# Transposed scores in two column halves, in a two-layer gated attention and feed-forward kernel

## The reference

```python
# _L0_xattn_ref, bs = 16, sq = sk = 64
q = (query @ wq).reshape(bs, sq, 32, 128).transpose((0, 2, 1, 3))
k = (key @ wk)  # 8 heads, each repeated for 4 query heads
v = (value @ wv)
q = _apply_rope(q, 0)
k = _apply_rope(k, 0)
raw = jnp.einsum('bhqd,bhkd->bhqk', q, k) / scale
masked = raw + mask[:bs, None, 0:sq, :sk]
attn = jax.nn.softmax(masked, axis=-1)
out = jnp.einsum('bhqk,bhkd->bhqd', attn, v)
...
return out @ wo
# caller
x = x + jnp.tanh(g_xattn[0]) * _L0_xattn_ref(_layernorm(x), ctx, ctx, mask, ...)
x = x + jnp.tanh(g_ffn[0]) * _L0_ffn_ref(_layernorm(x), ...)    # 4-bit weights, 8-bit activations
x = x + jnp.tanh(g_xattn[1]) * _L1_xattn_ref(_layernorm(x), ctx, ...)
x = x + jnp.tanh(g_ffn[1]) * _L1_ffn_ref(_layernorm(x), ...)    # experts picked by index `active`
```

## Time and profile before

| what | us |
|---|---|
| median of 3 runs (lowest, highest) | 801.29 (799.98, 801.77) |
| the profiled execution, whole | 801.0 |
| its span in the trace | 799.0 |
| PE busy | 788.0 |
| DVE busy | 586.8 |
| ACT busy | 446.9 |
| POOL busy | 503.3 |
| PE busy in the span from 300 to 560 us | 259.39 of 260.00 |

### The profile page before, as it was taken

How to read it: one execution, slowest core, us unless ns; L and a number is a source line. 1 busy time by engine, 2 the same in 40 slices (tenths; PEclk the granted TensorE clock), 3 DMA queues, 4 the chain that set the end, 5 groups by cost and what they waited for, 6 DMA issues and landing times.

```text
span 799.0 us, 13826 instructions
## 1 busy us (share of the span) xinstructions
PE 788.0 (99%) x5060; PEld 645.4 (81%) x5060; DVE 586.8 (73%) x1097; ACT 446.9 (56%) x844; POOL 503.3 (63%) x429
## 2 busy tenths in 40 slices
PE   8999999999999999999999999999999999999997
PEld 7888888888888888888888888888765777777776
DVE  5867988668888654686666565565899988998873
ACT  4754555444445434444445443333579898888773
POOL 1697577745766764566666456645457885887762
PEclk9999999999999999999999999999999999999999
DMA  9411331432333231733212110166273413213101
GB/s 304 134 67 47 98 94 41 126 77 57 93 90 91 63 102 31 52 90 93 87 40 68 49 45 27 33 75 251 90 190 100 107 48 86 67 48 80 48 15 40
DMA packets 72258, 66.76 MB, mean 84 GB/s; under 512 B 35920, under 2 KB 51504, under 8 KB 71808
## 3 DMA queue, kind: packets, MB, share of 16 engines
q1 hardware_dynamic: 71520, 65.56, 31.8%
q10 hardware_dynamic: 672, 0.33, 0.1%
HBM read 49.04 MB, written 6.34 MB: 69 GB/s over the span
## 4 chain that ended last, share of the span: by engine, by line
PE 93%; DVE 4%; ACT 1%; POOL 1%; DMA 1%; issue 1%; SPq 0%; DVEq 0%
PE bank L87 12%; PE bank L88 11%; PE bank L89 11%; PE bank L532 7%; PE bank L527 7%; PE bank L528 7%; PE bank L509 7%; PE bank L653 4%; PE bank L1660 4%; PE bank L1646 3%; PE bank L1612 2%; PE bank L1583 2%; PE bank L1591 2%; PE bank L640 2%; PE bank L1636 2%; PE bank L1637 2%
## 5 line engine op out<-in xcount | busy, mean ns | idle before, releaser
L963 DVE SCALAR_TENSOR_TENSOR x_res<-bank,gate,x_res 128x512 f32<-128x512 f32 x128 | 94.1, 744 | 67.6 <-PE bank L532 67.3
L1249 POOL TENSOR_TENSOR prob<-prob,row_inv 128x512 f32<-128x512 f32 x32 | 33.5, 1048 | 162.4 <-DVE row_inv L959 162.4
L1235 POOL TENSOR_TENSOR rope_swap<-rope_swap,trig 128x512 f32<-128x512 f32 x80 | 105.9, 1323 | 35.0 <-ACT rope_swap L722 34.7
L721 ACT COPY rope_swap<-bank 64x512 f32<-64x512 f32 x80 | 46.8, 585 | 106.8 <-DVE rope_cos L934 106.7
L87 PE MATMUL bank<-xnT_hi,wq_hi 128*128 128x512 f32 x256 | 103.0, 402 | 0.0
L527 PE MATMUL bank<-wo_hi,oT_hi 128*128 128x512 f32 x256 | 101.7, 397 | 1.2 <-DVE x_res L963 0.6
L88 PE MATMUL bank<-xnT_lo,wq_hi 128*128 128x512 f32 x256 | 101.4, 396 | 0.0
L89 PE MATMUL bank<-xnT_hi,wq_lo 128*128 128x512 f32 x256 | 101.2, 395 | 0.0
L528 PE MATMUL bank<-wo_lo,oT_hi 128*128 128x512 f32 x256 | 100.8, 394 | 0.0
L934 DVE TENSOR_TENSOR rope_cos<-bank,trig 128x512 f32<-128x512 f32 x80 | 54.6, 682 | 61.2 <-PE bank L89 61.1
L1241 POOL TENSOR_TENSOR q_rope<-rope_cos,rope_swap 128x512 f32<-128x512 f32 x64 | 84.4, 1319 | 5.0
(11 more groups left out here) (259 smaller groups left out, 2017.8 us busy)
## 6 DMA issues: line engine op xcount, KB each, us to landing
wq_raw<-in_L_xattn_wq SPq DMA_DIRECT2D x16, 512.0 KB, 4.2
wo_raw<-in_L_xattn_wo SPq DMA_DIRECT2D x16, 512.0 KB, 3.9
xn<-in_L_ffn_Wd SPq DMA_DIRECT2D x16, 256.0 KB, 3.2
b_ctx<-in_ctx SPq DMA_DIRECT2D x32, 128.0 KB, 2.6
b_k_twice<-b_qk_hi SPq DMA_DIRECT2D x32, 128.0 KB, 2.4
w_T_dram<-w_out SPq DMA_DIRECT2D x28, 128.0 KB, 2.7
w_T<-w_T_dram SPq DMA_DIRECT2D x2, 1376.0 KB, 17.9
xn<-in_L_ffn_Wg SPq DMA_DIRECT2D x10, 256.0 KB, 3.8
```

What stands on the lines that cost most here:

```text
L963: dve.scalar_tensor_tensor(out=K.x[:, t, :], in0=wo_ps[t % 2][:, :], scalar=K.gate[:, 0:1], in1=K.x[:, t, :], op0=ALU.mult, op1=ALU.add).t ...
L1235: pool.tensor_tensor(out=sw, in0=sw, in1=sin_b, op=ALU.mult).then_inc(s_rope, 1)
```

## The change

It has four parts.

- Scores of units 1 to 31 (`scoreT_unit`) are computed transposed: the stationary operand is now `k_rope` of one batch (64 columns wide), the moving one the 128 query rows. Even batches write partitions 0 to 63 of the bank, odd ones 64 to 127. ScalarE then copies the bank to SBUF (`prob_flat`), and TensorE transposes it back in four 128 by 128 transposes (`score_transposes`) behind the values product and the weight transposes, ahead of the items. Unit 0 stays as it was (`first_scores`).
- On VectorE `times_cos` of a slot's first item comes between the two halves of `oT_lo`, and `second_piece` (weight quantisation) ahead of the other items' `times_cos`.
- On GpSimd the rotation of a slot's first item comes ahead of `normalise`.
- On VectorE the selection of experts moves from ahead of `soft_first` to the end of slot 30.

The semaphore `s_score` is now counted twice for each unit, and `s_probT_sb` too. The core of the diff:

```diff
+        prob_flat = [p[:, :, :, :].rearrange("p t b k -> p (t b k)") for p in prob]
...
-            def score_unit(G, jp, u):
...
+            def scoreT_unit(G, jp, u):
 
                 U = 4 * G + 2 * jp + u
                 need = [("q", 1, u), ("k", u)] if jp == 0 else [("Q", 1, u)]
                 pe.wait_ge(s_rope, 2 * max(rope_of(G, pos_of(G, *i)) for i in need) + 2)
-                if U > 0:
-                    pe.wait_ge(s_soft, 5 * (U - 1) + 1)
-                for n in range(2 * UT):
-                    b = 2 * UT * u + n
-                    mm = pe.matmul(score[:, n * S:(n + 1) * S], q_rope[jp][:, b], k_rope[:, b * S:(b + 1) * S],
-                                   start=True, stop=True)
+                pe.wait_ge(s_soft, 5 * (U - 1) + 1)
+                for tl in range(UT):
+                    for par in range(2):
+                        b = 2 * (UT * u + tl) + par
+                        mm = pe.matmul(score[par * S:(par + 1) * S, tl * P:(tl + 1) * P], k_rope[:, b * S:(b + 1) * S],
+                                       q_rope[jp][:, b].rearrange("p h s -> p (h s)"), start=True, stop=True)
+                mm.then_inc(s_score, 1)
+
+            def score_transposes(U):
+                pe.wait_ge(s_probT_sb, 2 * U)
+                for tl in range(UT):
+                    mm = pe.transpose(score[:, tl * P:(tl + 1) * P], prob_flat[U % 2][:, tl * P:(tl + 1) * P], K.ident[:, :])
                 mm.then_inc(s_score, 1)
@@ PE, slot
                 if U < 2 * NPAIR - 1:
-                    score_unit(g if (jp, u) != (1, UNITS - 1) else g + 1, *next_unit(jp, u))
-                pe.wait_ge(s_probT_sb, U + 1)
+                    scoreT_unit(g if (jp, u) != (1, UNITS - 1) else g + 1, *next_unit(jp, u))
+                pe.wait_ge(s_probT_sb, 2 * U + 1)
...
                 weight_transposes(pair_at(U))
+                if U < 2 * NPAIR - 1:
+                    score_transposes(U + 1)
                 for G, pos in items:
                     item(G, pos)
@@ ACT, body: ahead stand shift, wq_piece, wk_piece, wv_piece
                     if U > 0:
                         probT_copy(U)
+                    if U < 2 * NPAIR - 1:
+                        act.wait_ge(s_score, 2 * U + 2)
+                        act.copy(prob_flat[(U + 1) % 2], score[:, :]).then_inc(s_probT_sb, 1)
                     if U == 2 * NPAIR - 1:
                         base_high_part(1)
                     act.wait_ge(s_av, U + 1)
@@ DVE, slot
-                if U == 2 * NPAIR - 2:
-                    selection_of_experts()
-                    selection_matrices()
                 if U < 2 * NPAIR - 1:
                     soft_first(U + 1)
...
+                oT_low(U, 0)
+                if items and ITEMS[items[0][0]][items[0][1]][0] != "v":
+                    times_cos(*items[0])
+                oT_low(U, 1)
                 if U < 2 * NPAIR - 1:
                     soft_sum(U + 1)
                 if U == 2 * NPAIR - 2:
                     qk_w_low_part()
                     base_low_part(0)
-                for k, (G, pos) in enumerate(items):
+                    selection_of_experts()
+                    selection_matrices()
+                second_piece(U)
+                for G, pos in items[1:]:
                     if ITEMS[G][pos][0] != "v":
                         times_cos(G, pos)
-                    if k == 0:
-                        second_piece(U)
-                if not items:
-                    second_piece(U)
@@ POOL, body
-                    if U < 2 * NPAIR - 1:
-                        normalise(U + 1)
+                    if not items:
+                        if U < 2 * NPAIR - 1:
+                            normalise(U + 1)
                     for k, (G, pos) in enumerate(items):
                         if ITEMS[G][pos][0] != "v":
                             rotate(G, pos)
+                        if k == 0:
+                            normalise(U + 1)
```

More of the change, by code:

```diff
@@ L498, in item, with first_scores @@
                     mm.then_inc(s_proj, 1)
-            def score_unit(G, jp, u):
+            def first_scores():
+                pe.wait_ge(s_rope, 2 * max(rope_of(0, pos_of(0, *i)) for i in [("q", 1, 0), ("k", 0)]) + 2)
+                for b in range(2 * UT):
+                    mm = pe.matmul(score[:, b * S:(b + 1) * S], q_rope[0][:, b], k_rope[:, b * S:(b + 1) * S],
+                                   start=True, stop=True)
+                mm.then_inc(s_score, 1)
+            def scoreT_unit(G, jp, u):
                 U = 4 * G + 2 * jp + u
@@ L629, in _ @@
             item(0, 9)
-            score_unit(0, 0, 0)
+            first_scores()
             item(0, 10)
@@ L941, in soft_first @@
                 pr = prob[u][:, :, :, :].rearrange("p t b k -> p (t b) k")
-                dve.wait_ge(s_score, U + 1)
+                dve.wait_ge(s_score, 2 * U + 1)
                 dve.scalar_tensor_tensor(out=pr, in0=score[:, :].rearrange("p (b k) -> p b k", k=S),
@@ L1139, in statistics_end, with oT_low @@
                 dve.tensor_scalar(K.var_eps[:, 0:UT], K.meanvar[:, 0:UT, 1], EPS, None, ALU.add).then_inc(s_x_stat, 1)
+            def oT_low(U, par):
+                dve.wait_ge(s_oT_hi, 2 * U + 2)
+                dve.tensor_tensor(out=oT_lo[:, :, :, par, :],
+                                  in0=av[par][:, :].rearrange("p (t h q) -> p t h q", t=UT, h=2),
+                                  in1=f32(oT_hi[:, :, :, par, :]), op=ALU.subtract).then_inc(s_oT_lo, 1)
             def slot(g, last, jp, u, U, items):
@@ L1161, in slot @@
                     router_offset()
-                dve.wait_ge(s_oT_hi, 2 * U + 2)
-                for par in range(2):
-                    dve.tensor_tensor(out=oT_lo[:, :, :, par, :],
-                                      in0=av[par][:, :].rearrange("p (t h q) -> p t h q", t=UT, h=2),
-                                      in1=f32(oT_hi[:, :, :, par, :]), op=ALU.subtract).then_inc(s_oT_lo, 1)
+                oT_low(U, 0)
+                if items and ITEMS[items[0][0]][items[0][1]][0] != "v":
+                    times_cos(*items[0])
+                oT_low(U, 1)
                 if U < 2 * NPAIR - 1:
```

## The result

| what | before | after |
|---|---|---|
| median of 4 runs each (lowest, highest), us | 800.7 (799.98, 801.77) | 808.16 (806.6, 808.9) |
| ratio after / before, 95% interval | | 1.009 [1.0078, 1.0102] |
| span of the profiled execution | 799.0 | 806.9 |

A forecast was written before the change was run, and what follows sets the result against it. TensorE, busy 788.0 of 799.0 us, was taken as the bound. Terms 1 to 5 summed as -8.4 + 1.5 + 1.8 + 0.6 + 3.3 = -1.2, giving a forecast of 800.0 us, range 795.5 to 805.5.

The forecast's parts named there:

- Term 1: Score block on TensorE: narrower scores, less the transposes back, save 0.28 us a slot, 8.4 over 30 slots.
- rival C: Between scores and values product: switching from column to row halves drains more; 807.6 us at 0.25 a slot; chance 0.20.
- B: Rival on TensorE's tiling switches: they are cheaper, saving 0.40 a slot, time 796.5 us; chance 0.24.
- D: Rival on the score matmuls: the two column halves don't overlap at all, time 826.5 us; chance 0.04.
- Term 2: Slot 0: ScalarE's weight casts stand ahead of the new score copy, so TensorE waits; cost 1.5 us, bounds 1.2 to 1.8.
- Term 4: Slot 9: the last rotation comes later and the scores wait for it; cost 0.6 us, bounds 0 and 0.7.
- Term 3: Slots 28 to 30: scores wait 0.94 us for GpSimd's last rotation, 0.88 more than before; slots 28 and 29 cost 1.8.
- Term 5: Slot 30, bound by VectorE: cost 3.3 us, of which the uncovered selection is 1.6; bounds 2.0 to 3.6.

The follow-up runs named there:

- later low half of wo: Kernel before with turned scores and new orders in 27 slots, GpSimd's low half of wo behind the second rotation in slots 27 to 29: 797.5 us, ratio 0.9935.
- orders only: Kernel before with only the new orders on VectorE and GpSimd; scores and selection as before: 809.24 us, ratio 1.0092.
- selection back: Changed kernel with the selection of experts back ahead of the softmax of slot 30: 805.54 us, ratio to before 1.0046.
- GpSimd waiting: Changed kernel with GpSimd's subtractions for the context's low halves made to wait until the selection is done: 809.34 us, slot 30 14.51.
- the other kernel with such stores: Kernel with 27 turned slots, with the store of the first two weights' scales cut into ten from slot 14 on: 802.41 us, ratio to before 1.0002.

## Why the prediction was wrong

- **Term 1, the score block: right.** The scores took 1.02 and the transposes ahead of them 0.53, as worked out, the transposes back 0.41, and an ordinary slot became 0.29 to 0.36 shorter where 0.28 was forecast. The values product and its entry cost what they did, so rival C, a dearer switch from columns to rows, did not happen: that its 807.6 lies near the measured 808.16 is chance. B's 0.40 was not reached, and D is out. Slots 3 to 5 and 10 gave only a third of it; in them VectorE's second piece was stretched as in slot 2.
- **Term 2, slot 0: right,** 1.40 of wait for ScalarE against 1.5. **Term 4: too small,** 1.01 of wait against 0.6, beyond its bound of 0.7.
- **Term 3: right in size,** a wait of 0.78 against 0.94, with one step of its working not borne out. It let `times_cos` start up to 1.38 earlier, held only by VectorE's order. With the orders alone, where no later softmax takes this back, the working would leave no wait, and there was one of 0.79: `times_cos` waited for the first item itself (1.19 in slot 27 of that kernel). In the whole change the later softmax takes most of the 1.38 back anyway, so the omission did not show.
- **Term 5, slot 30: this step failed.** It took the selection at the 1.6 of the earlier trace rows, where GpSimd ran only short `iota` and memset operations beside it, and did not ask what ran beside its new place. Now it ran beside GpSimd's context low halves and took 3.7. The rest of the chain was right: with GpSimd out of the way slot 30 was 14.51, and the forecast had 14.6. The sum also had no term for the clock: it let T of slot 31 follow `accumulate` by 3.67, and it was 6.09. Together 4.4 of the 9.1 by which the sum missed the difference of the spans (7.9 + 1.2).
- **Slot 2: not seen.** The text weighed GpSimd's margins and ScalarE's, and of VectorE's second piece it asked only what comes later for being behind it, not what runs beside it. The piece took 4.0 instead of 2.5, TensorE waited 1.91 and then ran at the lower level for a while: 3.6 of the miss.
- The Trainium skill, page "SBUF — State Buffer", section "SBUF: two separate sides", offers a mechanism: VectorE and GpSimd share one pair of SBUF ports as an exclusive lock, and a VectorE operation in a two-port mode, or with two SBUF inputs beside a GpSimd operation that reads SBUF, waits until the GpSimd operation that holds it is over. The traces agree in the times: 0.17 became 1.18 and 0.42 became 1.51, and both ended with or 0.3 behind GpSimd's operation. No run here shows the ports themselves.
- The remainder, about 1.1, is start-up and tail (0.8) and slots 3 to 5, 9, 10 and 16 (1.7 together), less what the ordinary slots gained beyond 0.28 (0.8) and what term 3 cost less (0.5).

## What to carry to other kernels

When an operation moves, look up what another engine does at its new place; its duration of the old place holds only for the old neighbours. Price a wait of TensorE, even one as short as the 0.78 here, with a possible stretch at the 1.2 GHz level on top, here 1.2 to 2.4 us, and give it as a range that starts at 0, since it came and stayed away behind equal waits. A change that helps in most slots and hurts in a few should be made in most slots: together with the later low half of wo, that turned +7.5 into -4.6.

## What was not expected of the hardware

- A VectorE operation on 4 elements a partition took 1.18 instead of 0.17 beside a GpSimd subtraction, and one on 512 took 1.51 instead of 0.42 beside a GpSimd rotation.
- The TensorE level fell to 1.2 GHz behind waits of 0.78 (orders only, slot 29), 1.91 (after, slot 2) and 3.93 (after, slot 30), and not behind 0.78 (after, slot 28), 1.92 (selection back, slot 2) and 1.91 (GpSimd waiting, slot 30). The wait's length alone does not decide.
- Behind stores of 4-byte elements the DMA engines were 0.92 busy at 8 GB/s, and the slot of this stretch became 5.0 us longer (7.0 in the other kernel with such stores). With the stores spread over more slots and SyncE held back the kernel took 813.6 against 802.5.
- Column halves of fp32 matmuls overlap as well between other work as in the second layer: 16 records in 1.02 from their start to that of the values product.
